# Two transformer layers on one core: the order of the opening, and a share of the weight scaling and of the softmax normalization moved from VectorE to GpSimd

## The reference

```python
x = x + L0_xattn(layernorm(x), ctx, ctx)           # 16 heads of 16
x = x + L0_ffn(layernorm(x))                       # gate, up, down, 704 hidden
x = x + L1_xattn(layernorm(x), ctx, ctx, mask)     # 16 heads of 64
x = x + L1_ffn(layernorm(x))                       # 1024 hidden
```

```python
scores = einsum('bhqd,bhkd->bhqk', Qh, Kh) / scale
attn = softmax(scores - max(scores))
attn = clip(attn, 1e-12, None)
attn = attn / sum(attn)
ctx = einsum('bhqk,bhkd->bhqd', attn, Vh)
```

## Time and profile before

| | us |
|---|---|
| median of 3 runs (lowest, highest) | 927.66 (927.36, 927.87) |
| profiled execution, its own time | 927.82 |
| its span, first to last instruction | 926.0 |
| TensorE busy | 900.5 (97%) |
| VectorE busy | 669.8 (72%) |
| ScalarE busy | 602.1 (65%) |
| GpSimd busy | 204.6 (22%) |

### The profile page before, as it was taken

The page is one execution under the profiler, slowest core; times in us unless marked ns, Lnnn a source line. Parts: engine busy times, 40 slices in busy tenths (PEclk is TensorE's granted clock), DMA queues, the critical chain, the costliest instruction groups (busy, mean ns, idle before and its releaser), DMA issues.

```text
span 926.0 us, 16209 instructions
## 1 busy us (share of the span) xinstructions
PE 900.5 (97%) x5610; PEld 601.8 (65%) x5610; DVE 669.8 (72%) x2179; ACT 602.1 (65%) x1671; POOL 204.6 (22%) x316
## 2 busy tenths in 40 slices
PE   6899999999999999999999999999999999999998
PEld 3555576767665567576675566667757655757786
DVE  5999883763989786475598978367478988837568
ACT  3888425972789643795378953499257984269845
POOL 3211001862000000486000000077400000028600
PEclk9999999999999999999999999999999999999999
DMA  9500000000000000000000010000000000000000
GB/s 294 212 1 2 29 1 23 2 1 1 1 1 25 1 28 24 1 1 2 1 0 8 18 29 1 24 1 1 1 0 1 19 7 1 1 0 2 2 1 23
DMA packets 14560, 18.35 MB, mean 20 GB/s; under 512 B 3088, under 2 KB 11664, under 8 KB 14480
## 3 DMA queue, kind: packets, MB, share of 16 engines
q1 hardware_dynamic: 12288, 15.40, 5.0%
q10 hardware_dynamic: 2064, 1.91, 0.7%
q0 software_dynamic: 128, 0.01, 0.0%
HBM read 15.21 MB, written 2.10 MB: 19 GB/s over the span
## 4 chain that ended last, share of the span: by engine, by line
PE 76%; DVE 13%; ACT 8%; issue 3%; DMA 1%; SPq 0%; DVEq 0%; ACTq 0%
PE bank L1243 28%; PE bank L1258 10%; PE bank L1526 6%; PE bank L1624 6%; PE bank L1506 6%; PE bank L1358 5%; PE bank L1414 4%; ACT ring L671 4%; DVE row_max L1050 3%; PE bank L1391 3%; PE bank L1481 1%; PE bank L1492 1%; PE bank L1251 1%; PE bank L1430 1%; ACT ring L715 1%
## 5 line engine op out<-in xcount | busy, mean ns | idle before, releaser
L463 POOL TENSOR_TENSOR rstd<-var_eps,minus_half 128x2 f32<-128x2 f32 x32 | 23.3, 734 | 533.1 <-DVE var_eps L886 533.1
L481 POOL TENSOR_TENSOR ring<-ring,row_inv 128x256 f32<-128x256 f32 x192 | 112.1, 613 | 95.4 <-DVE row_inv L1145 95.4
L556 ACT ACTIVATE ring<-bank 128x512 f32<-128x512 f32 x224 | 123.6, 612 | 14.1 <-PE bank L1258 12.6
L1258 PE MATMUL bank<-ident_s,ring 128*128 128x128 f32 x768 | 105.0, 279 | 5.1 <-DVE ring L1058 2.7
L1258 PEld LDWEIGHTS bank<-ident_s,ring 128*128 128x128 f32 x768 | 82.8, 141 | 39.2 <-issue 15.7
L715 ACT ACTIVATE ring<-ring,row_max 128x256 f32<-128x256 f32 x192 | 95.1, 497 | 17.3 <-DVE row_max L1138 17.3
L671 ACT ACTIVATE ring<-bank,row_max 128x256 f32<-128x256 f32 x192 | 88.4, 496 | 5.7 <-DVE row_max L1050 5.7
L1138 DVE CUSTOM_DVE_ANT_0 ring<-bank,maskbias 128x256 f32<-128x256 f32 x192 | 70.7, 420 | 23.4 <-issue 23.4
L1050 DVE TENSOR_REDUCE row_max<-bank 128x2 f32<-128x512 f32 x128 | 79.4, 684 | 5.9 <-PE bank L1391 5.2
L1243 PE MATMUL bank<-wgu_s,act_s 128*128 128x352 f32 x256 | 78.4, 459 | 0.0
L1243 PE MATMUL bank<-ctxT_s,wk_s 128*128 128x512 f32 x160 | 76.4, 600 | 0.0
(11 more groups left out here) (192 smaller groups left out, 1753.3 us busy)
## 6 DMA issues: line engine op xcount, KB each, us to landing
x_s<-x SPq DMA_DIRECT2D x4, 512.0 KB, 3.9
ctxT_s<-ctxT SPq DMA_DIRECT2D x4, 512.0 KB, 4.2
w_s<-w SPq DMA_DIRECT2D x2, 1024.0 KB, 16.3
out<-act_s SPq DMA_DIRECT2D x16, 128.0 KB, 1.7
wk_s<-wk SPq DMA_DIRECT2D x1, 1024.0 KB, 13.4
wv_s<-wv SPq DMA_DIRECT2D x1, 1024.0 KB, 14.7
wq_s<-wq SPq DMA_DIRECT2D x1, 1024.0 KB, 16.2
wo_s<-wo SPq DMA_DIRECT2D x1, 1024.0 KB, 17.5
```

What stands on the lines that cost most here:

```text
L481: ins = pool.tensor_tensor(probs1[i % PRING1][:, a, :], probs1[i % PRING1][:, a, :], row_inv[:, i, a:a + 1].to_broadcast([P, SEQ]), ALU.mult)
L556: act.activation(probsT[u % TRING][:, :, :].rearrange("p a q -> p (a q)"), psum(at, key)[:], ACT.Copy).then_inc(drain(at, key), 1)
L1258: ins = pe.transpose(psum(at, key)[:, c * SEQ + a * P:c * SEQ + (a + 1) * P], tile[:, a, c * P:(c + 1) * P], ident_s[:])
```

## The change

1. TensorE's front: input transposes first (as soon as the layernorm is done), then first keys, queries, scores of round 0, and only then second keys and values. The banks are moved for it: second keys to bank 7, queries to banks 5 and 6.
2. ScalarE follows: inputs, first keys, `piece_steps(0)`, queries; second keys are evacuated between the exponentials of units 1 and 2.
3. VectorE does the maxima of round 0 ahead of the scaling of piece 1.
4. For pieces 1 to 4 GpSimd divides (`divide_piece`, a product with the inverse scale); VectorE multiplies the inverse scale (32 to 48 columns) by the constant that the division had carried. `wscaled` counts one more step for each of these.
5. In every group GpSimd normalizes the third unit of each round (`normalize0`); VectorE still takes its inverse sums. TensorE waits for it on a semaphore of its own, `clipped0_pool`.
6. GpSimd's order in the opening: division of piece 1 ahead of `b1` and `bias_x`; then in each round the third unit, followed by a product (even rounds) or the division of the next piece (odd rounds), and `mask_to_bias` in round 1 after the division.

```diff
+POOL_UNIT = 2
@@ banks
-        jobs.add(("k0", c), c)
+        jobs.add(("k0", c), c if with_last_layer else 7 * c)
-        jobs.add(("q0", c), c if with_last_layer else 7 * c)
+        jobs.add(("q0", c), c if with_last_layer else 5 + c)
@@ counts
+def scaled_before(n):
+    return SCALE_OPS * n + sum(k in POOL_PIECES for k in range(n))
+def normalized0(u):
+    return u // 4 + 1 if u % 4 == POOL_UNIT else u + 1 - (u + 3 - POOL_UNIT) // 4
@@ gpsimd
+            def divide_piece(n):
+                nb = weight_pieces[n].shape[-1] // BLOCK
+                blocks = weight_pieces[n].rearrange("p (b e) -> p b e", b=nb)
+                pool.wait_ge(wscaled, scaled_before(n) + SCALE_OPS)
+                pool.tensor_tensor(blocks, blocks, inv_scale[:, 0:nb].unsqueeze(2).to_broadcast([P, nb, BLOCK]), ALU.mult).then_inc(wscaled, 1)
+            def normalize0(g, u):
+                pool.wait_ge(inv0, g * UNITS + u + 1)
+                for a in range(2):
+                    ins = pool.tensor_scalar(probs0[u % PRING0][:, a, :], probs0[u % PRING0][:, a, :], row_inv[:, u, a:a + 1], CLIP,
+                                             ALU.mult, ALU.max)
+                ins.then_inc(clipped0_pool, 1)
             ln_power(0)
+            divide_piece(1)
             pool.wait_ge(rest_loaded, 16 * 5)
             pool.tensor_scalar(b1_s[:], b1_s[:], UNITS_OF_FIX, None, ALU.mult).then_inc(b1_scaled, 1)
             pool.wait_ge(max0, 1)
             bias_x(0)
-            for n in POOL_PIECES:
-                if n == 2:
+            for r in range(ROUNDS0):
+                normalize0(0, 4 * r + POOL_UNIT)
+                if r % 2 == 0:
+                    multiply_piece(POOL_PIECES[r // 2])
+                elif r // 2 + 2 in POOL_PIECES:
+                    divide_piece(r // 2 + 2)
+                if r == 1:
                     pool.wait_ge(mask_loaded, 16)
-                    pool.wait_ge(max0, 9)
                     mask_to_bias()
-                multiply_piece(n)
             for g in range(GROUPS - 1):
...
                 ln_power(g * 4 + 4)
+                for r in range(ROUNDS0):
+                    normalize0(g + 1, 4 * r + POOL_UNIT)
@@ scalar
             def piece_steps(n):
-                act.wait_ge(wscaled, SCALE_OPS * (n + 1))
+                act.wait_ge(wscaled, scaled_before(n + 1))
...
                         for i in round_units0(r):
+                            if i == 2 and with_weights:
+                                layer0_keys(at, [1])
                             exponentials(i)
...
             act.wait_ge(keys_loaded, 16 * 4)
+            layer0_inputs(opening_pass)
+            layer0_keys(opening_pass, [0])
             piece_steps(0)
-            layer0_keys(opening_pass, [0])
-            layer0_inputs(opening_pass)
-            layer0_keys(opening_pass, [1])
@@ vector
-                dve.scalar_tensor_tensor(blocks_of(src, nb), blocks_of(src, nb), TIES_DOWN, inv.unsqueeze(2).to_broadcast([P, nb, BLOCK]),
-                                         ALU.mult, ALU.mult).then_inc(signal, 1)
+                if divided:
+                    dve.scalar_tensor_tensor(blocks_of(src, nb), blocks_of(src, nb), TIES_DOWN, inv.unsqueeze(2).to_broadcast([P, nb, BLOCK]),
+                                             ALU.mult, ALU.mult).then_inc(signal, 1)
+                else:
+                    dve.tensor_scalar(inv, inv, TIES_DOWN, None, ALU.mult).then_inc(signal, 1)
...
                     dve.reciprocal(row_inv[:, u, :], row_sum[:, u, :]).then_inc(inv0, 1)
+                    if u % 4 == POOL_UNIT:
+                        return
...
                         if g is None:
+                            scale_piece(1)
                             dve.wait_ge(values_loaded, 16 * 2)
                             layer0_values(at, range(TILES))
...
             round_piece(0)
-            scale_piece(1)
@@ tensor
                 for u in units:
-                    pe.wait_ge(clipped0, group * UNITS + u + 1)
+                    if u % 4 == POOL_UNIT:
+                        pe.wait_ge(clipped0_pool, group * ROUNDS0 + normalized0(u))
+                    else:
+                        pe.wait_ge(clipped0, group * (UNITS - ROUNDS0) + normalized0(u))
...
-            pe.wait_ge(wk0_packed, 1)
-            pe.wait_ge(ctx_loaded, 16)
-            layer0_keys(opening_pass, [0])
             pe.wait_ge(ident_loaded, 16)
             for h in range(HALVES):
                 pe.wait_ge(xn_ready, 2 * h + 2)
                 transpose_xn(opening_pass, 0, h, xn0)
-            layer0_keys(opening_pass, [1])
+            pe.wait_ge(wk0_packed, 1)
+            pe.wait_ge(ctx_loaded, 16)
+            layer0_keys(opening_pass, [0])
             pe.wait_ge(wq0_packed, 1)
             layer0_queries(opening_pass)
+            layer0_scores(opening_pass, 0)
+            layer0_keys(opening_pass, [1])
             pe.wait_ge(values_loaded, 16 * 2)
-            layer0_scores(opening_pass, 0)
```

More of the change, by code:

```diff
@@ L348, in xattn_ffn_twice @@
         scaled, steps_ready, rounded = sem("scaled"), sem("steps_ready"), sem("rounded")
-        max0, inv0, clipped0 = sem("max0"), sem("inv0"), sem("clipped0")
+        max0, inv0, clipped0, clipped0_pool = sem("max0"), sem("inv0"), sem("clipped0"), sem("clipped0_pool")
         bias_ready, exp1, inv1, norm1 = (sem(n) for n in ("bias_ready", "exp1", "inv1", "norm1"))
@@ L827, in blocks_of, with quantize_scale @@
                 return ap.rearrange("p (b e) -> p b e", b=nb)
-            def quantize_scale(src, signal, k):
-                n, done = src.shape[-1], SCALE_OPS * k
+            def quantize_scale(src, signal, done, divided=True):
+                n = src.shape[-1]
                 nb = n // BLOCK
@@ L857, in quantize @@
             def quantize(src, k, between=None):
-                quantize_scale(src, scaled, k)
+                quantize_scale(src, scaled, SCALE_OPS * k)
                 if between is not None:
@@ L870, in scale_piece @@
                     dve.wait_ge(wrounded, ROUND_OPS * n)
-                quantize_scale(weight_pieces[n], wscaled, n)
+                quantize_scale(weight_pieces[n], wscaled, scaled_before(n), n not in POOL_PIECES)
             def round_piece(n):
```

## The result

The changed kernel takes 938.82 us (median of 4 runs, 938.55 to 939.52) against 927.76 (927.36 to 927.91): ratio 1.0121, 95% interval 1.0109 to 1.0133, 11.1 us slower. Its profiled execution has a span of 937.0 against 926.0. The forecast was 930.9, range 925.5 to 935.0: the right side, a third of the size, and outside the range.

What follows compares the result with a forecast made beforehand. It took TensorE to be three quarters of the chain, with VectorE bounding part of the opening; -0.3 (front) - 0.2 + 0.4 (divisions) + 3.3 (third unit) = +3.2 us on 927.82, so 930.9 for the median, range 925.5 to 935.0.

Steps and rivals of the forecast that it cites:

- Point 3: Third unit of each round on GpSimd: holds VectorE's next normalization in opening and crossings, +3.3 us.
- 11c: VectorE held c = 0.3 us by GpSimd's pair, six times in crossings, five in the opening: +3.3 us.
- The hold itself: VectorE's `tensor_scalar` of unit 3 starts 0.3 us before GpSimd is through with unit 2, and is held.
- Point 1: Front of the opening: TensorE 3 us earlier, VectorE 1.15 us earlier; less a 0.83 hold, -0.3 us stays.
- What is late next: GpSimd in the opening: `bias_x` moves to about 25.4 to 27.75, on top of the first normalizations; 0.83 us taken once.
- rival C: In the opening `bias_x` holds the first normalization to its end: 1.4 us more than the forecast, 932.3; chance 0.10.
- the 0.82 of the earlier trace: Hold read from two VectorE normalizations beside GpSimd's mask bias, 1178 and 1232 ns; basis for the 0.83 taken for `bias_x`.
- Point 2: Divisions of later pieces on GpSimd: -0.2 at piece 2, +0.4 at piece 4; bounds -0.8 and +1.2 us.
- The -0.2 at piece 2: Opening: unit 11's normalization would end at 46.3 against 46.46, the stretch turning from VectorE's to ScalarE's.
- piece 4's `piece_steps`: Opening: piece 4's division would end at 73.0 where ScalarE had taken it at 72.57, delaying exponentials: +0.4 us.
- B: Rival: GpSimd's pair is longer than a product; at 0.85 us each, 8.8 us of holds, 936.4; chance 0.13.

Runs made afterwards that it cites:

- e5: Changed kernel with the third unit normalized by GpSimd's tensor_tensor product, clip left out, instead of its tensor_scalar: 934.23 us, ratio 1.0068.
- e2: Kernel before with only the new order of the front, no division and no unit on GpSimd: 929.87 us, ratio 1.0022.
- e8: e2 with three useless 512-column products on TensorE ahead of the first transposes: 930.82 us, ratio 1.0025.
- e4: Changed kernel with three useless 512-column products on TensorE between the values and the first transposes: 936.9 us, ratio 1.0098.
- e9: e2 with `bias_x` moved to where round 4's maxima begin: 928.74 us, ratio 1.0011.
- e10: e9 with two useless 256-column products ahead of the last values' product: 928.19 us, ratio 1.0002.
- e7: Kernel before with only the divisions of pieces 1 to 4 on GpSimd: 928.39 us, ratio 1.0007.
- e12: Kernel before with only the third unit of each round normalized on GpSimd: 934.67 us, ratio 1.0074.
- e1: Changed kernel with VectorE normalizing all units again: 931.36 us, ratio 1.0039.
- e6: Changed kernel with another GpSimd form for the third unit by group (product, one-operation tensor_scalar, two operations with an immediate): one execution, 935.00 us.
- e3: Changed kernel with `bias_x` ahead of the division of piece 1 on GpSimd: 936.14 us, ratio 1.0096.

## Why the prediction was wrong

- **Point 3, the third unit: mis-sized, and by another mechanism.** I priced GpSimd's `tensor_scalar` by its product, 613 ns, capped it at 0.85 and let it cost only by holding VectorE, 11c = 3.3. It takes 1.15, and the pair's 2.29 closes a loop of its own in every round. I had written that beyond 0.85 TensorE would wait for unit 2 itself in every round, and put no time and no chance on it; that is what happened, 6.3 in the crossings and 0.6 in the opening, though the bound is nearer 1.0 than 0.85. The hold itself was forecast right, 0.3 for the pair of unit 3 (0.91 against 0.61), and cost nothing since the chain no longer went there. The mask bias's 2.7 ns a column was the row of the same operation; I took the row of the same type. It would not have been enough either: it makes 0.69 of 256 columns.
- **Point 1, the front: VectorE was as forecast to the third of a microsecond** (24.99 against 25.3; maxima 19.15 against 19.35), in part by luck, since with e5's warm-up the same step came at 26.53. What is late next was named: `bias_x` over the first normalization. The size was wrong, 0.83 for 2.07: the held pair ended with `bias_x` itself, rival C. And the 0.82 of the earlier trace rows was misread. It is no fixed length. The normalization of 1178 ns is the first of this pair of before, and it ended at 44.04, when the mask bias had ended at 43.89:

```profile
42.86 1.43 DVE L1058 TENSOR_SCALAR ring<-ring,row_inv 128x256 f32<-128x256 f32 x2
```

  So one of the two rows behind the 0.82 already spoke for C; only the other, in the layernorm, ended well before the mask bias did. The page "SBUF — State Buffer" of the Trainium skill (Who interferes with whom) had said the whole instruction, and for `bias_x` the traces agree three times: 2422 ns here, 0.96 in e2, 1.55 in e8, each ended with `bias_x`. For GpSimd's `tensor_scalar` they agree in part: the mask bias held the normalization to its end in before and in the changed kernel (47.42 for 47.28), but not the layernorm's, and a pair of 2.29 held VectorE's pair by 0.3.
- **What I had not seen at all: the clock.** I counted 3 us earlier on TensorE and 1.15 on VectorE and did not ask what TensorE does in between. It idles, and after it the clock fell, in seven of the profiles. e4 puts 1.9 us on that in the changed kernel, the two groups of e8 about 2, e9 against e10 only 0.55. I had not seen either that the new order puts the length of the warm-up on VectorE's path, up to 1.6 us between profiles.
- **Point 2, divisions: right in the main.** +0.2 forecast, +0.6 measured, within its bounds, and piece 4's `piece_steps` at 73.06 in e7 where 73.0 was worked out. The -0.2 at piece 2 did not come: in e7 the normalization of unit 11 ended at 46.49, against 46.46, because VectorE waited 1.00 us for the exponentials and then met the mask bias as before.
- **The sum.** 6.9 for units (e12), 0.6 for divisions (e7), which leaves 3.6 for the front together with its hold and the clock; 1.9 of that is the clock (e4). In the profiles the first transposes start 0.46 later than before (27.77 against 27.31): the hold of 2.1 took back the 1.65 that the front had brought. The other 1.2 is not assigned by any run. How much of the 3.6 would stay with a warm-up of another length is open.
- **The range** left out B's upper side, where the time was: the longest value that I allowed for an instruction without a row was one that I had set myself.

## What to carry to other kernels

Before an operation goes to another engine, measure that operation on that engine: the same multiplication took 0.59 us as a product and about 1.0 as a `tensor_scalar` there, and 1.15 with the clip. Then find the length from which it bounds the loop: here the last 0.2 of a pair cost more than all the rest. Work that leaves an engine off the chain gives nothing back, while the hand-over adds its own length to the loop of a round. And when one engine is moved ahead, look at how long it then stands still: the idle time in front of a long stretch of products can cost more than the move brings, and at what the moved work now waits for.

## What the runs showed of the hardware

- A GpSimd `tensor_tensor` with both inputs in SBUF held a VectorE `tensor_scalar` on SBUF to its own end, even one of 48 columns (0.19 to 1.55 us in e8). The mask bias, a `tensor_scalar` of GpSimd, held one to its own end as well (44.04 for 43.89 before, 47.42 for 47.28 after), but not the one at 208.3. VectorE's reductions from PSUM and its sum of PSUM and SBUF ran beside it at full speed (1.55 for four).
- GpSimd's `tensor_scalar` on 256 float columns took 0.97 to 1.15 us in its three forms (half a pair of 1.93 to 2.29), its product 0.59. The Trainium skill's "GPSIMD Engine Reference" (Engine selection) calls one-input work roughly line-rate; the traces disagree.
- In the profiles TensorE's granted clock was at 0.50 after 1.88 to 3.34 us without work in front of the first transposes (the changed kernel, e1, e2, e5, e6, e9), after 2.18 in front of e8's useless products, and after 1.88 and 1.89 in front of the output product (e6, e5). It stayed at 1.00 after 1.24 to 1.28 at the first place (before, e3, e7, e10 to e12) and after 1.73 at the last (all others but e4). The order is not strict: in e6 it fell once more after 1.66, near 48.7.
- The stretch at 0.50 lasted 6.8 us in the changed kernel and in e1, 3.4 at every place in e2, e5, e6, e8 and e9.
- The same warm-up code took from 5.12 to 6.71 us in different executions. Its weight loads change from 0.34 us to 0.19 on the way, at 10.07 in the changed kernel and at 11.90 in e2. What starts the full pace sooner or later stays open: the granted clock's column does not show it.
